# Eight sandwiched layers on one core: attention scores two tiles ahead, a norm one batch later, a clamp on GpSimd and experts' up products three units ahead

## The chip, the cores and the metric

One core of a Trainium2 chip runs the whole network in one program. The metric is the device time of that program in microseconds: the median of three runs.

## The reference

`x` has 8 sequences of 512 tokens of width 128, all in float32. Each of eight layers computes `x = x + layernorm(f(layernorm(x)))`. The `f` are, in order:

0. attention with 16 heads of width 8, RMS-normed queries and keys, and a causal window of 32 tokens
1. a gated ternary layer: `silu(x·w1·s1) * (x·w2·s2)`, two square layers of width 512 with GELU, and a last product to width 128
2. causal attention with one head
3. 32 experts, the best 4 of each token, width 128: `glu = min(a, 7)`, `lin = clip(b, -7, 7)`, `glu * sigmoid(1.702 glu) * (lin + 1)`
4. a gated delta rule with its own feed-forward layer
5. 8 experts, best 2, width 512, `silu(a) * b`
6. full attention with rotated positions
7. 8 experts, best 2, width 512, ReLU

## The kernel before

Each layer is a stage: a block in which five engines run their own instruction streams, tied by semaphores, with a barrier at its end. A batch is one sequence: `B = 8`, of `TB = 4` tiles of 128 tokens. The stream `x` stays in SBUF through all stages. There is no planner: the order on every engine is written out by hand, and every wait is in program order, so what stands behind a waiting instruction waits too. Between VectorE instructions that depend on each other, `Chain.link` (L47) adds a wait on the engine's own semaphore.

**Layer norms.** `Norm.dve_stats` (L127) takes statistics on VectorE, `pool_rstd` (L140) the power -0.5 on GpSimd, and `dve_apply` (L147) applies both on VectorE. `Post.dve_add` adds the normed result to `x`.

**Stage 0, `stage_attn0`** is unrolled over 32 tiles `n = 4b + t`. Per tile: `scores` on TensorE into PSUM banks 0 and 1 (L1006); `masked` on VectorE (L1199 adds the mask, L1202 takes the maxima); `shifted` on GpSimd (L946); `probs`, the exp, on ScalarE (L1120); `transposes` on TensorE (L1015); `probs_turned` on ScalarE (L1124); `values` on TensorE (L1028); `weighted` on VectorE. Around them the next batch is prepared: `turn_input`, `project`, `unscaled`, `squares`, `mean_squares`, `roots`, `scaled` (L1192), `turn` (L986), `queries`, `keys` (L1107, eight copies of 128x512), `project_v`, and batch b-1's output is projected and added (`result`, L1213). `scores(n+1)` is issued one tile ahead of `transposes(n)`. Banks 2 and 3 serve the projections, the turns and the output in turn.

**Stage 1, `stage_ffn0`** loops over batches. TensorE: eight up products (L354, a pair of 128x512 halves of w1 and w2 for each of four `m`, in banks 0 to 3), then two square layers of 16 products each (L363), between them the transposes of the next batch's normed input, and at last 16 products of 128x128 (L376). ScalarE: silu (L401) and GELU (L409). VectorE: the gated product (L443), then the next batch's first norm, then the wait for L376, the scaling (L451), the post norm and the add to `x` (L293), and only then the next batch's first gated product.

**Stages 3, 5 and 7, `stage_moe`** loop over batches, with 32 units unrolled in each. A unit is one 128-wide slice of hidden width: `up(u + LAG)`, two products of 128x512 (L607; one in the ReLU kind), then `down(u)`, four products of 128x128 (L617). `LAG` is 2. Four PSUM banks hold two units of up products. The routing and norms of the next batch are put between units (`AT_...`). In stage 3 every unit is an expert, so VectorE adds every unit's result into `acc` (`collect`, L784, four instructions). The nonlinearity of stage 3 is: ScalarE ta (L708), tc (L710), tb (L713); VectorE td = (ta - 7)*tc (L811) and, on the same engine, the clamp tb = min(tb - 8, 6) (L812); GpSimd h = td*tb (L544). In stage 5 it is one ScalarE and one VectorE instruction.

Of the kernel before, what the change touches and what calls it, by code (L numbers as in the profile page):

```python
# [164 lines left out]
class Pre:  # L165
# [62 lines left out]

    def dve_second(self, v, ch, b):
# [75 lines left out]
def stage_ffn0(core):  # L305
# [11 lines left out]
    free = [s(f"bank{i}_free") for i in range(4)]  # L317
    t_ready = [s(f"silu{i}_ready") for i in range(2)]
# [4 lines left out]
    with nc.Block() as block:  # L323
# [5 lines left out]
        def _(g):  # L329
# [3 lines left out]
            with g.Fori(0, B) as b:  # L333
                ch.reset()
                pre.pool(g, ch, b + 1)
                post.pool(g, ch)

        @block.tensor
        def _(pe):
            st.wait_loads(pe)  # L340
            pre.seed_pe(pe)
            for i in range(3):
                pe.sem_inc(h_free[i], 1)
            pre.pe(pe, 0)
            with pe.Fori(0, B) as b:
                pe.wait_ge(pre.xT_ready, 1)
                pe.sem_clear(pre.xT_ready)
                xb = c.xT[:, bass.ds(b * L, L)]
                for m in range(HC):
                    for k, w in enumerate((w1, w2)):  # L350
                        i = (2 * m + k) % 4
                        pe.wait_ge(free[i], 1)
                        pe.sem_clear(free[i])
                        pe.matmul(c.ps[i][:], w[:, m * P:(m + 1) * P], xb, start=True,  # L354
                                  stop=True).then_inc(ready[i], 1)
                for n, w in enumerate((h1, h2)):
# [11 lines left out]
                    if n == 0:  # L368
                        pre.pe(pe, b + 1)
                pe.wait_ge(h_ready[2], HC)  # L370
# [9 lines left out]
            for i in range(4):  # L380
                pe.wait_ge(free[i], 1)
                pe.sem_clear(free[i])
            pe.wait_ge(y_free, 1)
            pe.sem_clear(y_free)
            pre.drain_pe(pe)

        @block.scalar
        def _(a):
# [3 lines left out]
            a.sem_inc(free[2], 1)  # L392
            pre.act(a, 0)
            with a.Fori(0, B) as b:
                for m in range(HC):
                    i = 2 * m % 4
                    a.wait_ge(ready[i], 1)
                    a.sem_clear(ready[i])
                    a.wait_ge(t_free[m % 2], 1)
                    a.sem_clear(t_free[m % 2])  # L400
                    a.activation(t_s[:, m % 2, :], c.ps[i][:], ACT.Silu, scale=s1[:, m:m + 1]).then_inc(t_ready[m % 2], 1)  # L401
                    a.drain().then_inc(free[i], 1)
                for n, sc in enumerate((g1, g2)):
# [8 lines left out]
                    if n == 0:  # L412
                        pre.act(a, b + 1)
            pre.drain_act(a)
# [8 lines left out]
        def _(v):  # L423
# [8 lines left out]
            pre.dve(v, ch, 0)  # L432
            with v.Fori(0, B) as b:
                ch.reset()
                v.wait_ge(h_free[0], 1)
                v.sem_clear(h_free[0])
                for m in range(HC):
                    i = (2 * m + 1) % 4
                    v.wait_ge(ready[i], 1)
                    v.sem_clear(ready[i])  # L440
                    v.wait_ge(t_ready[m % 2], 1)
                    v.sem_clear(t_ready[m % 2])
                    v.scalar_tensor_tensor(hid[0][:, m, :], c.ps[i][:], s2[:, m:m + 1], t_s[:, m % 2, :],  # L443
                                           ALU.mult, ALU.mult).then_inc(h_ready[0], 1)
                    d = v.drain()
                    d.then_inc(free[i], 1)
                    v.sem_inc(t_free[m % 2], 1)
                pre.dve(v, ch, b + 1)
# [4 lines left out]
                v.sem_inc(y_free, 1)  # L453
                post.dve_stats(v, ch, lambda t: y[:, t, :])
                post.dve_add(v, ch, b, lambda t: y[:, t, :])
            pre.drain_dve(v)
            v.wait_ge(h_free[0], 1)
            v.sem_clear(h_free[0])
# [15 lines left out]
LAG, DEPTH = 2, 4  # L474


def stage_moe(core, tag, E, topk, inner, eps, residual, kind):
# [4 lines left out]
    FC = UNITS // E  # L482
    relu, silu, glu7 = kind == "relu", kind == "silu", kind == "glu7"
# [33 lines left out]
    td_ready = [s(f"td{i}_ready") for i in range(DEPTH)]  # L517
    y_ready = [s(f"y{i}_ready") for i in range(2)]
# [9 lines left out]
    with nc.Block() as block:  # L528
# [5 lines left out]
        def _(g):  # L534
# [12 lines left out]
            for u in range(LAG):  # L547
                hidden(u)
            with g.Fori(0, B) as b:
                ch.reset()  # L550
                for u in range(UNITS):
# [6 lines left out]
                    hidden((u + LAG) % UNITS)  # L558
# [4 lines left out]
        def _(pe):  # L563
# [71 lines left out]
            for u in range(LAG):  # L635
                up(u, c.xT[:, 0:L])
            with pe.Fori(0, B) as b:
                xb, xb_next = c.xT[:, bass.ds(b * L, L)], c.xT[:, bass.ds((b + 1) * L, L)]
                for u in range(UNITS):
# [8 lines left out]
                    if u + LAG == UNITS:  # L648
                        next_batch()
                    up((u + LAG) % UNITS, xb if u + LAG < UNITS else xb_next)  # L650
                    down(u)
            for u in range(LAG):
# [18 lines left out]
        def _(a):  # L671
# [22 lines left out]
            def front(u):  # L694
# [9 lines left out]
                if silu:  # L704
# [5 lines left out]
                a.activation(tc[:, j, :], ta[:, j, :], ACT.Sigmoid, scale=-1.702, bias=c1[:])  # L710
# [3 lines left out]
                             scale=-1.0).then_inc(t_ready[j], 1)  # L714
                a.drain().then_inc(a_free[2 * k + 1], 1)

            for u in range(LAG):
                front(u)
            with a.Fori(0, B) as b:
                ch.reset()  # L720
                for u in range(UNITS):
# [6 lines left out]
                    front((u + LAG) % UNITS)  # L728
# [3 lines left out]
        def _(v):  # L732
# [65 lines left out]
            def front(u):  # L798
# [9 lines left out]
                if glu7:  # L808
                    v.wait_ge(t_ready[j], 1)
                    v.sem_clear(t_ready[j])  # L810
                    v.scalar_tensor_tensor(td[:, j, :], ta[:, j, :], 7.0, tc[:, j, :], ALU.subtract, ALU.mult)  # L811
                    v.tensor_scalar(tb[:, j, :], tb[:, j, :], 8.0, 6.0, ALU.subtract, ALU.min).then_inc(td_ready[j], 1)  # L812
# [25 lines left out]
            for u in range(LAG):  # L838
# [2434 lines left out]
```

## Time and profile before

| | |
|---|---|
| median of 3 runs | 6248.97 us (6245.62 to 6252.19) |
| profiled execution | 6221.95 us, span 6220.1 us |
| stage 0, from 11 to 381 us | 370 us |
| stage 1, from 381 to 762 us | 381 us |
| stage 3, from 888 to 1755 us | 867 us |
| stage 5, from 4568 to 5307 us | 739 us |
| VectorE's L1199 of tiles 12 and 16 | start at 180.18 and 221.21 us |
| last L1199 of stage 0 | starts at 361.15 us |

The stages end in a barrier, so the time is the sum of the stages, and each has its own limit. Whole-program busy shares mix them; they are read in windows of one batch.

### The profile page before, as it was taken

The page shows a single profiled execution, that of the slowest core. Times are in us where ns is not written, and L with a number is a line of the kernel's source. Part 1 is how long each engine was busy: PE and PEld are TensorE (multiplying, and loading weights), DVE is VectorE, ACT ScalarE, POOL GpSimd, SP SyncE. Part 2 cuts the span into 40 slices and gives each one's busy share as a digit, 9 for nine tenths or more (in the row PEclk, how much of TensorE's full clock was granted, in tenths as well). Part 3 has the DMA queues.
Part 4 walks back from the last instruction along what each step waited for, and adds up shares of the span by engine and source line. Part 5 has one row for each costly group of instructions (what it writes and reads, how often), then busy time and mean ns, then how long its engine had stood idle before and what let it go on. Part 6 is the DMA issues. An engine that isn't in the chain of part 4 may idle for free. (4 is left out here: it accounts for less than half of the span.)

```text
span 6220.1 us, 182529 instructions
## 1 busy us (share of the span) xinstructions
PE 5232.3 (84%) x72132; PEld 3776.6 (61%) x72132; DVE 3558.8 (57%) x9531; ACT 2288.6 (37%) x4072; POOL 2504.0 (40%) x2788
## 2 busy tenths in 40 slices
PE   4568868888848888898888888898679999787998
PEld 2334345555536777777777777777346666576776
DVE  4631268787865565555565565565545545685333
ACT  3532236666623333333333333333222333111333
POOL 1210014444436666666666666666300000573000
PEclk8789989999969999999999999999789999898999
DMA  0000010000000000000000000000010000000000
GB/s 19 2 20 0 2 42 1 0 0 0 0 7 11 11 11 12 12 13 12 11 12 11 11 12 11 11 12 11 7 42 0 0 0 0 4 1 28 0 0 13
DMA packets 29562, 58.05 MB, mean 9 GB/s; under 512 B 7312, under 2 KB 14240, under 8 KB 28704
## 3 DMA queue, kind: packets, MB, share of 16 engines
q1 hardware_dynamic: 28960, 48.86, 2.6%
q8 instruction: 520, 8.52, 0.6%
q14 instruction: 82, 0.67, 0.0%
HBM read 46.75 MB, written 2.10 MB: 8 GB/s over the span
## 5 line engine op out<-in xcount | busy, mean ns | idle before, releaser
L617 PEld LDWEIGHTS psum<-m_wd,m_h 128*128 128x128 f32 x6144 | 805.6, 192 | 485.4 <-issue 484.3
L617 PE MATMUL psum<-m_wd,m_h 128*128 128x128 f32 x6144 | 819.6, 277 | 95.3 <-remote 69.6
L2183 POOL TENSOR_TENSOR e_kd<-e_kd,e_tail 128x512 f32<-128x512 f32 x325 | 368.7, 1135 | 567.7 <-PE psum L2290 554.2
L607 PE MATMUL psum<-xT,m_wa 128*128 (+1 forms) x1032 | 544.3, 610 | 8.4 <-remote 8.4
L607 PE MATMUL psum<-xT,m_wb 128*128 (+1 forms) x1032 | 532.8, 598 | 0.0
L784 DVE SCALAR_TENSOR_TENSOR m_acc<-psum,m_combine,m_acc 128x128 f32<-128x128 f32 x1440 | 403.3, 342 | 224.0 <-PE psum L617 211.0
L544 POOL TENSOR_TENSOR m_h<-m_td,m_tb 128x512 f32<-128x512 f32 x258 | 328.6, 1274 | 468.6 <-DVE m_tb L812 468.6
L2320 PE MATMUL psum<-e_T,e_N 64*64 64x32 f32 x10400 | 407.1, 232 | 67.7 <-remote 66.3
L2320 PEld LDWEIGHTS psum<-e_T,e_N 64*64 64x64 f32 x10400 | 370.6, 148 | 113.2 <-issue 110.0
L2290 PE MATMUL psum<-e_kd,e_k 64*64 64x64 f32 x10400 | 420.1, 237 | 0.3
L143 POOL TENSOR_SCALAR m_post_rstd<-m_post_mv 128x4 f32<-128x4 f32 x27 | 6.2, 228 | 990.7 <-DVE m_post_mv L133 990.7
L2290 PEld LDWEIGHTS psum<-e_kd,e_k 64*64 64x64 f32 x10400 | 372.4, 149 | 6.9 <-issue 1.2
L805 DVE SCALAR_TENSOR_TENSOR m_h<-psum,m_bb,m_ta 128x512 f32<-128x512 f32 x258 | 193.2, 749 | 308.4 <-ACT m_ta L705 305.2
L607 PEld LDWEIGHTS psum<-xT,m_wb 128*128 128x128 f32 x1032 | 199.3, 193 | 253.5 <-issue 253.5
L705 ACT ACTIVATE m_ta<-psum,m_ba 128x512 f32<-128x512 f32 x258 | 177.2, 687 | 458.9 <-PE psum L607 458.8
L2341 PE MATMUL psum<-e_Z,e_TT 64*64 64x32 f32 x8320 | 296.7, 221 | 25.0 <-DVE e_Z L2693 21.1
L2585 ACT ACTIVATE e_T<-psum 128x256 f32<-128x256 f32 x325 | 125.6, 386 | 514.4 <-PE psum L2341 514.4
L2693 DVE COPY e_Z<-psum 64x256 f32<-64x256 f32 x325 | 135.9, 418 | 301.8 <-PE psum L2320 301.5
L2341 PEld LDWEIGHTS psum<-e_Z,e_TT 64*64 64x64 f32 x8320 | 267.5, 135 | 48.7 <-issue 33.5
L699 ACT ACTIVATE m_h<-psum,m_ba 128x512 f32<-128x512 f32 x258 | 177.3, 687 | 288.3 <-PE psum L600 288.3
L2177 POOL TENSOR_TENSOR e_k<-e_k,e_tail 128x256 f32<-128x256 f32 x390 | 281.2, 721 | 0.0
L600 PE MATMUL psum<-m_normed,m_wa 128*128 128x512 f32 x516 | 268.9, 604 | 6.2 <-remote 6.2
(434 smaller groups left out, 11884.4 us busy)
## 6 DMA issues: line engine op xcount, KB each, us to landing
e_w<-in_e_w SPq DMA_DIRECT2D x66, 321.0 KB, 2.9
m_wa<-in_m_wa SPq DMA_DIRECT2D x12, 512.0 KB, 7.5
m_wd<-in_m_wd SPq DMA_DIRECT2D x12, 512.0 KB, 8.7
m_wb<-in_m_wb SPq DMA_DIRECT2D x8, 512.0 KB, 8.8
f_h<-in_f_h SPq DMA_DIRECT2D x2, 1024.0 KB
out<-x SPq DMA_DIRECT2D x1, 2048.0 KB, 8.7
f_w<-in_f_w SPq DMA_DIRECT2D x3, 256.0 KB
g_w<-in_g_w SPq DMA_DIRECT2D x3, 256.0 KB
```

The source lines that it names most:

```text
L544: g.tensor_tensor(h[:, j, :], td[:, j, :], tb[:, j, :], ALU.mult).then_inc(h_ready[j], 1)
L600: pe.matmul(c.ps[u % 4][:], wa[q][:, j, :], nrm[:, e % 2, :], start=True, stop=True).then_inc(a_ready[u % 4], 1)
L607: pe.matmul(c.ps[i][:], w[q][:, j, :], xb, start=True, stop=True).then_inc(a_ready[i], 1)
L617: r = pe.matmul(c.ps[4 + e % 2][:, t * P:(t + 1) * P], h[:, u % DEPTH, t * P:(t + 1) * P], wd[u // UQ][:, u % UQ, :], start=(m == 0 and t ...
L699: a.activation(h[:, j, :], c.ps[u % 4][:], ACT.Relu, bias=ba[:, u:u + 1]).then_inc(h_ready[j], 1)
L784: r = v.scalar_tensor_tensor(to[:, t, :], c.ps[4 + e % 2][:, t * P:(t + 1) * P], comb[:, t, e:e + 1], acc[:, t, :], ALU.mult, ALU.add)
L805: v.scalar_tensor_tensor(h[:, j, :], c.ps[2 * k + 1][:], bb[:, u:u + 1], ta[:, j, :], ALU.add, ALU.mult).then_inc(h_ready[j], 1)
L2177: return g.tensor_tensor(even(k[:], m), even(src[:], m), gate, ALU.mult)
L2183: return g.tensor_tensor(both_odd(dst[:], m), both_odd(src[:], m), gate.unsqueeze(1).broadcast_to((P, 2, nb, m)), ALU.mult)
L2290: r = pe.matmul(c.psum[half(h), G_, chunk(u)], keys[half(h), chunk(u)], both_odd(gated[half(h), :, chunk(u)], 1 << l), start=True, stop=True)
L2320: r = pe.matmul(c.psum[half(1 - h), Z_, u * HC:(u + 1) * HC], N[half(h), l - 1, chunk(u)], even(T[half(h), chunk(u)], 1 << l), start=True, ...
L2341: r = pe.matmul(even(c.psum[half(h), T_, chunk(u)], 1 << l), left[half(h), chunk(u)], Z[half(h), u, :], start=False, stop=False, skip_grou ...
```

## The change

- Stage 0: `scores`, `masked` and `shifted` run two tiles ahead of `transposes` instead of one. Every step of the next batch is moved: `project` and `unscaled` to tile 3 of two batches before, `mean_squares`, `roots`, `scaled` and `turn` to tile 0, `queries` and `keys` to tile 1, `project_v` and `values` to tile 2. A batch's result, norm and add come two batches later instead of one. The input's transposes use bank 3.
- Stage 1: TensorE issues the first pair of up products of the next batch before L376 of this one; VectorE does the first gated product of the next batch at the end of the iteration; scaling, post norm and add of a batch are done in the next iteration, after its gated products.
- Stages 3 and 5: `up` runs three units ahead, with the same four banks and four buffers.
- Stage 3: the clamp is a GpSimd instruction ahead of the product, with a semaphore of its own from ScalarE. The wait of td no longer covers tb.

The core of the diff:

```diff
 stage_ffn0, TensorE
+            up(0, c.xT[:, 0:L])
             with pe.Fori(0, B) as b:
+                for m in range(1, HC):
+                    up(m, c.xT[:, bass.ds(b * L, L)])
...
+                up(0, c.xT[:, bass.ds((b + 1) * L, L)])
                 pe.wait_ge(h_ready[2], HC)
 stage_ffn0, VectorE
+            with v.Fori(1, B) as b:
+                ch.reset()
+                for m in range(1, HC):
+                    gated(m)
+                pre.dve_first(v, ch, b + 1)
+                scaled()
                 post.dve_stats(v, ch, lambda t: y[:, t, :])
+                pre.dve_last(v, ch, b + 1)
+                post.dve_add(v, ch, b - 1, lambda t: y[:, t, :])
+                first_gated()
 stage_moe
+    lag = 2 if kind == "relu" else 3
...
+                g.wait_ge(tb_ready[j], 1)
+                g.sem_clear(tb_ready[j])
+                ch.link(g.tensor_scalar(tb[:, j, :], tb[:, j, :], 8.0, 6.0, ALU.subtract, ALU.min))
                 g.wait_ge(td_ready[j], 1)
                 g.sem_clear(td_ready[j])
                 g.tensor_tensor(h[:, j, :], td[:, j, :], tb[:, j, :], ALU.mult).then_inc(h_ready[j], 1)
...
-                    v.tensor_scalar(tb[:, j, :], tb[:, j, :], 8.0, 6.0, ALU.subtract, ALU.min).then_inc(td_ready[j], 1)
 stage_attn0, TensorE
             for n in range(N):
                 b, t = n // TB, n % TB
+                if t == 3 and b + 2 < B:
+                    project(b + 2)
+                if n + 2 < N:
+                    scores(n + 2)
+                if t == 0 and b >= 2:
+                    output(b - 2)
                 if t == 2 and b + 1 < B:
+                    project_v(b + 1)
                 if n:
                     values(n - 1)
+                if t == 0 and b + 2 < B:
+                    turn_input(b + 2)
+                transposes(n)
                 if t == 0 and b + 1 < B:
+                    turn(b + 1)
+                if t == 3 and b:
+                    turn_output(b - 1)
 stage_attn0, ScalarE
                 if t == 1 and b + 1 < B:
                     queries(b + 1)
+                    keys(b + 1, range(2))
                 if n + 1 < N:
                     probs(n + 1)
                 if t == 0 and b + 1 < B:
+                    roots(b + 1)
...
+                    keys(b + 1, range(2, 6))
...
+                    values(b + 1)
...
+                    squares(b + 2)
+                probs_turned(n)
+                if t == 1 and b + 1 < B:
+                    keys(b + 1, range(6, HP))
 stage_attn0, VectorE
+                if t == 0 and b + 1 < B:
                     mean_squares(b + 1)
+                if t == 3 and b + 2 < B:
+                    unscaled(b + 2)
+                if n + 2 < N:
+                    masked(n + 2)
+                if t == 0 and b + 1 < B:
+                    scaled(b + 1)
                 if n:
                     weighted(n - 1)
+                if t == 0 and b >= 2:
+                    result(b - 2)
+                if t == 1 and b >= 2:
                     post.dve_stats(v, ch, lambda t: y[:, t, :])
```

## Rows read from the trace of the kernel before

**Rows 1.** The page's head, whole execution.

```profile
span 6220.1 us, 182529 instructions
...
PE 5232.3 (84%) x72132; PEld 3776.6 (61%) x72132; DVE 3558.8 (57%) x9531; ACT 2288.6 (37%) x4072; POOL 2504.0 (40%) x2788
```

**Rows 2.** Windows of one batch: block attention, ternary, clamped experts, silu experts.

```profile
core 0: us, PE busy (x) PEld busy (x) DVE busy (x) ACT busy (x) POOL busy (x), PEclk, DMA share, GB/s
180.18:221.21 41.03, 23.24 (x460) 15.20 (x460) 24.47 (x49) 20.62 (x25) 10.11 (x8) 0.79 0.00 1
533.41:577.82 44.41, 39.65 (x116) 18.93 (x116) 9.12 (x31) 11.41 (x15) 2.53 (x4) 1.00 0.00 0
1230.80:1333.60 102.80, 90.48 (x409) 55.96 (x408) 82.24 (x255) 68.15 (x103) 44.49 (x38) 0.98 0.00 0
4775.90:4863.50 87.60, 87.07 (x410) 55.81 (x409) 44.37 (x127) 26.63 (x38) 3.79 (x6) 1.00 0.00 0
```

**Rows 3.** Waits in that attention batch: total, times, longest (us).

```profile
PE psum L986 <- DVEq L1215: 6.5, 1, 6.5
...
PE psum L1006 <- ACT a_kz L1107: 5.9, 1, 5.9
```

**Rows 4.** Groups by line, that batch: busy us, mean ns, idle before.

```profile
L946 POOL TENSOR_TENSOR a_probs<-a_probs,a_max 128x1024 f32<-128x1024 f32 x4 | 7.6, 1900 | 30.6 <-DVE a_max L1202 30.6
...
L1199 DVE TENSOR_TENSOR a_probs<-psum,a_window 128x1024 f32<-128x1024 f32 x4 | 4.9, 1223 | 10.0 <-PE psum L1006 10.0
...
L155 DVE TENSOR_SCALAR a_post_z<-a_y,a_post_mv,a_post_rstd 128x128 f32<-128x128 f32 x4 | 1.1, 334 | 0.0
```

**Rows 5.** Timeline of a ternary batch: start, us, what, idle before.

```profile
538.48 0.69 DVE L293 TENSOR_TENSOR x<-x,f_post_z 128x512 f32 x1 [0.15 <-DVE f_post_z L155]
539.95 0.75 DVE L443 SCALAR_TENSOR_TENSOR f_hid<-psum,f_s,f_silu 128x512 f32<-128x512 f32 x1 [0.78 <-remote]
...
540.90 2.84 PE L354 MATMUL psum<-xT,f_w 128*128 x6 [2.10 <-DVEq L445]
...
543.58 13.90 PE L363 MATMUL psum<-f_hid,f_h 128*128 128x512 f32 x32
...
573.84 3.83 PE L376 MATMUL psum<-f_w,f_hid 128*128 128x128 f32 x32 [1.08 <-remote]
```

**Rows 6.** Groups by line in one batch of the clamped experts.

```profile
L544 POOL TENSOR_TENSOR m_h<-m_td,m_tb 128x512 f32<-128x512 f32 x32 | 40.8, 1274 | 55.6 <-DVE m_tb L812 55.6
L617 PE MATMUL psum<-m_wd,m_h 128*128 128x128 f32 x256 | 34.9, 280 | 11.8 <-remote 8.2 <-POOL m_h L544 3.6
L784 DVE SCALAR_TENSOR_TENSOR m_acc<-psum,m_combine,m_acc 128x128 f32<-128x128 f32 x124 | 34.7, 341 | 1.0 <-remote 0.7
...
L811 DVE SCALAR_TENSOR_TENSOR m_td<-m_ta,m_tc 128x512 f32<-128x512 f32 x32 | 22.2, 694 | 15.6 <-ACT m_tb L713 12.6 <-remote 2.8
...
L812 DVE TENSOR_SCALAR m_tb<-m_tb 128x512 f32<-128x512 f32 x33 | 13.8, 418 | 0.0
```

**Rows 7.** GpSimd's groups over the whole trace.

```profile
L2177 POOL TENSOR_TENSOR e_k<-e_k,e_tail 128x256 f32<-128x256 f32 x390 | 281.2, 721 | 0.0
...
L2193 POOL COPY e_hs<-xT 128x512 f32 (+1 forms) x66 | 40.5, 613 | 0.3 <-POOL e_N L2227 0.3
```

**Rows 8.** Timeline in the clamped experts, VectorE and GpSimd.

```profile
1242.65 2.11 DVE L155 TENSOR_SCALAR m_post_z<-m_done,m_post_mv,m_post_rstd 128x128 f32<-128x128 f32 x4
1242.90 1.27 POOL L544 TENSOR_TENSOR m_h<-m_td,m_tb 128x512 f32<-128x512 f32 x1 [1.05 <-DVE m_tb L812]
...
1251.97 0.23 POOL L143 TENSOR_SCALAR m_pre_rstd<-m_pre_mv 128x4 f32<-128x4 f32 x1
...
1252.28 1.04 POOL L144 TENSOR_TENSOR m_pre_rstd<-m_pre_rstd,mhalf 128x4 f32<-128x4 f32 x1
```

**Rows 9.** Timeline in the delta-rule stage, same two engines.

```profile
2640.52 0.69 DVE L2756 SCALAR_TENSOR_TENSOR e_kqn<-e_kn,e_be 128x512 f32<-128x512 f32 x1
2640.57 1.12 POOL L2177 TENSOR_TENSOR e_k<-e_k,e_tail 128x256 f32<-128x256 f32 x1
```

More of the change, by code:

```diff
@@ L317, in stage_ffn0 @@
     free = [s(f"bank{i}_free") for i in range(4)]
+    gate_ready = [s(f"gate{i}_ready") for i in range(2)]
     t_ready = [s(f"silu{i}_ready") for i in range(2)]
@@ L332, in _ @@
             pre.pool(g, ch, 0)
-            with g.Fori(0, B) as b:
+            pre.pool(g, ch, 1)
+            with g.Fori(1, B) as b:
                 ch.reset()
@@ L336, in _ @@
                 post.pool(g, ch)
+            post.pool(g, ch)
         @block.tensor
@@ L392, in _, with silu @@
             a.sem_inc(free[2], 1)
+            def silu(m):
+                i = 2 * m % 4
+                a.wait_ge(ready[i], 1)
+                a.sem_clear(ready[i])
+                a.wait_ge(t_free[m % 2], 1)
+                a.sem_clear(t_free[m % 2])
+                a.activation(t_s[:, m % 2, :], c.ps[i][:], ACT.Silu, scale=s1[:, m:m + 1]).then_inc(t_ready[m % 2], 1)
+                a.drain().then_inc(free[i], 1)
             pre.act(a, 0)
+            silu(0)
             with a.Fori(0, B) as b:
[L395 to L402, printed above, removed]
+                for m in range(1, HC):
+                    silu(m)
                 for n, sc in enumerate((g1, g2)):
@@ L413, in _ @@
                         pre.act(a, b + 1)
+                silu(0)
             pre.drain_act(a)
@@ L431, in _, with gated, first_gated, scaled @@
                 v.sem_inc(t_free[i], 1)
-            pre.dve(v, ch, 0)
-            with v.Fori(0, B) as b:
-                ch.reset()
+            def gated(m):
+                i = (2 * m + 1) % 4
+                v.wait_ge(gate_ready[i // 2], 1)
+                v.sem_clear(gate_ready[i // 2])
+                v.wait_ge(t_ready[m % 2], 1)
+                v.sem_clear(t_ready[m % 2])
+                v.scalar_tensor_tensor(hid[0][:, m, :], c.ps[i][:], s2[:, m:m + 1], t_s[:, m % 2, :],
+                                       ALU.mult, ALU.mult).then_inc(h_ready[0], 1)
+                d = v.drain()
+                d.then_inc(free[i], 1)
+                v.sem_inc(t_free[m % 2], 1)
+            def first_gated():
                 v.wait_ge(h_free[0], 1)
                 v.sem_clear(h_free[0])
[L437 to L448, printed above, removed]
+                gated(0)
+            def scaled():
                 v.wait_ge(y_ready, 1)
@@ L517, in stage_moe @@
     td_ready = [s(f"td{i}_ready") for i in range(DEPTH)]
+    tb_ready = [s(f"tb{i}_ready") for i in range(DEPTH)]
     y_ready = [s(f"y{i}_ready") for i in range(2)]
@@ L546, in _ @@
             pre.pool(g, ch, 0)
-            for u in range(LAG):
+            for u in range(lag):
                 hidden(u)
@@ L634, in _ @@
             next_batch()
-            for u in range(LAG):
+            for u in range(lag):
                 up(u, c.xT[:, 0:L])
@@ L837, in _ @@
                 make_normed(1, 0)
-            for u in range(LAG):
+            for u in range(lag):
                 front(u)
@@ L1132, in _ @@
             copy_input(0)
+            copy_input(1)
             squares(0)
@@ L1237, in _ @@
             masked(0)
+            masked(1)
+            unscaled(1)
+            input_stats(2)
+            input_norm(2)
             for n in range(N):
```

169 lines of the change are left out of this document (86 added, 83 removed).

## Prediction

> **What bounds the kernel now.** The page's head first [rows 1]: TensorE is busy 84% of the span, but that is a mean over stages with different limits, and each stage ends in a barrier. So I read windows of one batch in each stage that the diff touches [rows 2]. The reader is to see four different cases. In block attention (41.03 us a batch) no engine is busy more than 60%: VectorE 24.47, TensorE 23.24, ScalarE 20.62, GpSimd 10.11. The stage is bound by a chain. In the ternary layer (44.41 us) TensorE is busy 39.65: near its floor, with single gaps. In the clamped experts (102.80 us) TensorE has 90.48, VectorE 82.24, GpSimd 44.49. In the silu experts (87.60 us), whose TensorE work is almost the same, TensorE is busy 87.07 and never waits. That number is the floor for the clamped experts too.
>
> Then the waits inside each window. In attention VectorE waits 10.0 us in three of four tiles for the scores (L1199) [rows 4]; TensorE waits 6.5 us before it turns the queries and keys, and 5.9 us for the spread keys [rows 3]. One tile of lookahead doesn't cover scores, mask, maxima, 1.90 us on GpSimd and the exp, and the next batch's preparation stands in the same line. In the ternary layer TensorE has two gaps of a size: 2.10 us before the third up pair, since VectorE first ends the post norm (add at 538.48) and only then the first gated product at 539.95, and 1.08 us before L376, for the last GELU [rows 5]. In the clamped experts GpSimd's product waits 55.6 us a batch for the clamp on VectorE, and TensorE's L617 idles 11.8 us [rows 6].
>
> **Attention.** No instruction is added in a steady batch; the order changes. Scores get a whole tile more, so the 10.0 us at L1199 should go, save where the scores themselves are late. What is late next: `turn` waits for `scaled`, which follows the masked tile on VectorE, and the scores of the next tile are queued behind `turn` on TensorE; I take 2 us. The first scores of the next batch wait for all eight copied keys, which ScalarE interleaves with an exp and a turned tile: 2.5 us. Against 6.5 and 5.9 before [rows 3]. VectorE's own 24.47 plus 2 for handovers between dependent instructions is the floor under that: 24.5 + 2 + 2 + 2.5 = 31 us. TensorE's 23.24, at a mean clock of 0.79, stays under it [rows 2]. 41.03 - 31 = 10 us for each of the seven batches that prepare a next one: -70. The end pays: one more batch's result, statistics, power, apply and add stand after the last tile (the apply is 1.1 us [rows 4], the power 1.04 and the add 0.69 [rows 5, 8]), about 5 us, and about as much goes to the longer start. Attention: -60. Bounds: 26.5 us a batch (no stall left) gives -92; 35 us (the two key waits keep most of their length) gives -32.
>
> **Ternary layer.** The post norm moves behind the gated products, so 2.10 goes; the up pair, work that has to be done anyway, fills the 1.08 before L376, less some 0.3 for TensorE's drain ahead of it: -2.9 us a batch. VectorE's 9.12 busy us and GpSimd's 2.53 [rows 2] have 27 us of square products to hide under (two times 13.90 [rows 5]). Eight batches: -23. The first batch has no post norm in its way (+2.1), and after the last a pair of no use is computed: four instructions at 13.90/32 = 0.43 us, +1.7. Together -19; from -14 (the drain and the pair's start cost 1 us a batch) to -25.
>
> **Experts three units ahead.** Silu experts: TensorE never waits, so nothing is to be won. In both stages one more unit of the next, unused batch is computed: 4 * 0.43 = 1.7 us each, +3.4 together. Below nothing is excluded for the silu stage, since its batch is 100% TensorE.
>
> **The clamp.** VectorE loses 33 clamps, 13.8 us a batch [rows 6], and has 68.4 left. A unit's latency from up to down may now be three units instead of two, so bursts of routing and norms no longer stop TensorE at once. GpSimd gains 32 clamps of 128x512. No row shows that one. From below: the copy of 128x512, 613 ns [rows 7]; from above: the two-input product of the same size, 1274 ns [rows 6]. The clamp has one input like the copy and one more arithmetic step, so I take 0.65, nearest the copy. Then GpSimd has per unit 0.65 + 1.27, a link of 0.08 (from 1251.97 + 0.23 to 1252.28 [rows 8]) and some 0.15 for two waits: 2.15 us, times 32 = 69; three powers with their adds, 1.35 each, 4; 73.
>
> But VectorE and GpSimd don't run freely beside each other. Four applies that take 1.1 us [rows 4] took 2.11 beside a GpSimd product [rows 8], and GpSimd's 128x256 product, 721 ns on average [rows 7], took 1.12 us beside a VectorE instruction with two SBUF inputs [rows 9]. L811 is of that kind (ta and tc). So each unit's L811 costs GpSimd up to 0.4: 32 * 0.4 = 13, and norms and copies some 4. GpSimd: 90 us a batch, just over TensorE's floor of 87.6. With bursts not wholly hidden I take 93. (102.8 - 93) * 8 = -79. Bounds: the floor, -122; a clamp of 0.94, halfway to the product, adds 9.3 us: 102.3, or -4; at 1.27 with nothing overlapped, see the last rival.
>
> The Trainium skill, page "SBUF — State Buffer", section "Who interferes with whom", says that a VectorE instruction with two SBUF inputs and a GpSimd instruction that reads SBUF exclude each other for their whole length. Rows 9 agree in kind, with 0.4 us of 0.69 paid. The page speaks against this change: the clamp leaves VectorE's list but not the common resource; what that gives when taken whole is the first rival. The skill's "GPSIMD Engine Reference", section "Engine selection", calls one-input instructions there roughly line-rate; by that the clamp would be an estimated 0.43 us and a start cost, near my 0.65, and no run here shows it yet.
>
> **Sum.** -60 - 19 + 3.4 - 79 = -155, from the profiled execution's 6221.95 us (span 6220.1 and 1.9 around it): 6067. The median of the runs is 27 us above the profiled one, so 6249 - 155 = 6094 us.
>
> **Rivals.**
> 1. *The pair excludes itself wholly.* Per unit 0.69 (L811) + 0.65 + 1.27 + 0.23 gaps = 2.84; times 32 = 91, plus 4 for powers and 4 for norms: 99 us. The clamped experts give only -30: 6143 us. For it: rows 8 and 9. Against: in rows 9 part of GpSimd's start lay under the other's work.
> 2. *Attention's preparation still rules.* `scaled`, `turn`, keys and scores of a batch remain a line. Half of the 12.4 us of waits [rows 3] and the lookahead for nothing: 37.5 us a batch, -25 for the stage, 6129 us. For it: the waits of rows 3 are as long as L1199's. Against: each step has a tile of its own now.
> 3. *The lookahead does it all.* The clamped experts reach TensorE's floor, -122: 6051 us. For it: VectorE 68.4 and GpSimd 73 both lie under 87.6. Against: the overlap above.
> 4. *Slower.* The clamp on GpSimd costs as much as the product and overlaps nothing: 0.69 + 1.27 + 1.27 + 0.23 = 3.46 a unit, 111 + 8 = 119 us a batch, +128; with the other parts' -76, 6301 us. It decides from a batch of 112.3 us on, that is a clamp of 1.06 us. Against: the copy of 613 ns.
> 5. *It doesn't do what it says:* a new semaphore order makes TensorE wait elsewhere and all three stages stay within 0.2%. Little speaks for it, since TensorE's order does change.
>
> **How the numbers follow.** Chances: forecast 0.58, rival 1 0.16, rival 2 0.10, rival 3 0.09, rival 4 0.05, rival 5 0.02. The forecast's own range, from the bounds of its parts taken two at a time, is 6060 to 6130. To leave out no more than 2 in 10 the range has to reach past rivals 1 to 3, with the attention bound of -92 beside a part of rival 3 below: 6035 to 6185. Faster by over 0.2% (12.5 us, about what a measurement of this kernel can tell from no change) 0.93, within 0.02, slower 0.05.
>
> **What would show it.** In the changed profile: an attention batch (four L1199) of 28 to 34 us, with VectorE the busiest and L1199's wait mostly gone; TensorE's wait before `turn` near 2 us. A ternary batch of 41 to 42 us, with no gap over 0.5 inside the up products. A clamped batch of 90 to 96 us, a GpSimd clamp of 0.6 to 0.75 us, GpSimd busier than VectorE, L811 longer than its 694 ns where it meets GpSimd. A silu batch of 87.6 again. The prediction is wrong if the clamp takes over 0.95 us, if L811 and the product strictly alternate with gaps, or if attention stays over 36 us a batch.

## The result and the profile after

The changed kernel takes 6284.2 us (median of 4 runs, 6280.7 to 6289.0) against 6247.3 us before (4 runs, 6243.6 to 6252.2): a ratio of 1.0065, 95% interval 1.0049 to 1.0082. It is slower by 0.65%. The prediction was 6094 us, range 6035 to 6185, with 0.05 for slower. The sign was wrong.

The page's head and the row of the clamp, after:

```profile
span 6284.2 us, 183125 instructions
...
PE 5277.6 (84%) x72144; PEld 3773.8 (60%) x72144; DVE 3531.7 (56%) x9276; ACT 2292.1 (36%) x4078; POOL 3030.4 (48%) x3048
...
L588 POOL TENSOR_SCALAR m_tb<-m_tb 128x512 f32<-128x512 f32 x259 | 513.8, 1984 | 40.8 <-ACT m_tb L761 19.1
```

TensorE's busy time and share are almost those of [rows 1]. The new row is the case: the clamp on GpSimd takes 1.98 us on average. The stages, measured between barriers in both traces:

| stage | before | after | difference | predicted |
|---|---|---|---|---|
| 0, block attention | 369.7 | 327.0 | -42.7 | -60 |
| 1, ternary | 381.0 | 358.5 | -22.5 | -19 |
| 3, clamped experts | 867.2 | 989.3 | +122.1 | -79 + 1.7 |
| 5, silu experts | 739.0 | 741.1 | +2.1 | +1.7 |
| the others | | | +5.1 | 0 |

The sum is +64 of the two profiled spans. The profiled execution of before lay 25 us under its own median and that of after 2 us over its own, so the medians differ by 37. Of the others' +5.1, 7 us are in the delta rule (layer 4), whose code is the same. In the profiles of all the kernels with that code but the last one below it took 2605 to 2628 us (2619 before, 2626 after), so that is scatter. Three of the four parts went in the direction predicted; the fourth outweighs them.

Windows of one batch, after, in the order of [rows 2]:

```profile
core 0: us, PE busy (x) PEld busy (x) DVE busy (x) ACT busy (x) POOL busy (x), PEclk, DMA share, GB/s
164.35:198.01 33.66, 21.15 (x450) 14.42 (x452) 24.24 (x50) 20.31 (x25) 10.13 (x8) 0.85 0.01 2
616.50:657.80 41.30, 39.34 (x118) 19.09 (x117) 8.89 (x32) 11.42 (x15) 2.64 (x4) 1.00 0.00 0
1212.50:1330.30 117.80, 97.23 (x409) 55.62 (x408) 79.20 (x223) 68.13 (x102) 109.23 (x71) 0.97 0.00 0
4840.80:4928.40 87.60, 86.97 (x410) 55.71 (x409) 44.33 (x126) 26.64 (x38) 3.80 (x6) 1.00 0.00 0
```

A clamped batch takes 117.80 us and GpSimd is busy in 109.23 of them, against 44.49 before. VectorE went from 82.24 down to 79.20 only, for two reasons. The 13.8 us of clamps overlapped their neighbours on VectorE: with the clamps taken out of the trace of before, its busy time in that batch falls by 8.1 us. And a td takes 0.86 us on average instead of 694 ns [rows 6], 5.3 us a batch. The groups of that batch:

```profile
L588 POOL TENSOR_SCALAR m_tb<-m_tb 128x512 f32<-128x512 f32 x33 | 65.4, 1981 | 2.8
L591 POOL TENSOR_TENSOR m_h<-m_td,m_tb 128x512 f32<-128x512 f32 x32 | 41.2, 1288 | 5.6 <-remote 5.3 <-POOL m_tb L588 0.4
L664 PE MATMUL psum<-m_wd,m_h 128*128 128x128 f32 x256 | 37.6, 292 | 19.9 <-POOL m_h L591 16.5 <-remote 3.4
...
L859 DVE SCALAR_TENSOR_TENSOR m_td<-m_ta,m_tc 128x512 f32<-128x512 f32 x32 | 27.5, 860 | 27.7 <-ACT m_tc L757 25.0 <-remote 2.6
```

L588 is the clamp, L591 the product (L544 before), L664 `down` (L617 before), L859 td (L811 before). GpSimd now waits 8 us ahead of these two instructions where it waited 55.6 [rows 6]. TensorE waits 19.9 us ahead of `down` instead of 11.8, and 16.5 of it for GpSimd's product instead of 3.6. The timeline of one unit between bursts (a burst is the VectorE work of norm, routing or sum that stands between two units):

```profile
1082.73 1.92 POOL L588 TENSOR_SCALAR m_tb<-m_tb 128x512 f32<-128x512 f32 x1
...
1083.16 0.73 DVE L859 SCALAR_TENSOR_TENSOR m_td<-m_ta,m_tc 128x512 f32<-128x512 f32 x1 [1.39 <-ACT m_tc L757]
...
1084.83 1.27 POOL L591 TENSOR_TENSOR m_h<-m_td,m_tb 128x512 f32<-128x512 f32 x1 [0.18 <-remote]
...
1086.18 1.92 POOL L588 TENSOR_SCALAR m_tb<-m_tb 128x512 f32<-128x512 f32 x1
...
1086.25 1.15 PE L664 MATMUL psum<-m_wd,m_h 128*128 128x128 f32 x8 [0.57 <-POOL m_h L591]
```

Clamp 1.92, gap 0.18, product 1.27, gap 0.08: 3.45 us from one clamp to the next. 32 times that is 110.4 us, with the three powers 114. Clamps and products stretched beside VectorE (means of 1.98 and 1.29 us, for 1.92 and 1.27) add 3. TensorE's `down` starts 0.15 us after the product's end and had waited 0.57 us. VectorE's td (L859), which began 0.43 us into the clamp, took 0.73 us, hardly more than its 694 ns.

Attention, the waits of the batch of the first window:

```profile
PE psum L1042 <- DVEq L1276: 6.7, 1, 6.7
DVE a_probs L1260 <- PE psum L1062: 6.5, 2, 4.1
...
PE psum L1062 <- ACT a_kz L1164: 4.5, 1, 4.5
```

L1042 is `turn`, L1062 the scores, L1260 the mask's add. Before, the three were 6.5, 10.0 and 5.9 [rows 3, 4]. The batch went from 41.03 to 33.66, and the wait before `turn` is still there. Its timeline says what stands before it:

```profile
181.60 1.90 POOL L995 TENSOR_TENSOR a_probs<-a_probs,a_max 128x1024 f32<-128x1024 f32 x1 [3.07 <-DVE a_max L1263]
...
182.41 2.17 DVE L1253 TENSOR_TENSOR a_qk<-a_raw,a_rstd 128x1024 f32<-128x1024 f32 x1
...
185.46 0.69 DVE L1274 TENSOR_TENSOR a_y<-psum,a_bo 128x512 f32<-128x512 f32 x1
...
186.35 1.94 PE L1042 MATMUL psum<-ident,a_qk 128*128 128x128 f32 x8 [6.65 <-DVEq L1276]
```

`scaled` (L1253) took 2.17 us beside GpSimd's L995, where its median before was 1.44, and `turn` was released by the semaphore of L1276, behind L1274: that is `result`, which reads batch b-2's output out of PSUM bank 2 and so frees it for `turn`. VectorE's list places it behind `scaled` and `weighted`; it ended at 186.15.

Ternary layer, TensorE in one batch:

```profile
560.81 1.98 PE L359 MATMUL psum<-xT,f_w 128*128 x4 [0.53 <-remote]
...
562.63 3.73 PE L392 MATMUL psum<-f_w,f_hid 128*128 128x128 f32 x32
...
567.19 5.41 PE L359 MATMUL psum<-xT,f_w 128*128 x12 [0.82 <-remote]
```

Of the two gaps of [rows 5], 2.10 and 1.08 us, there are 0.53 us before the early pair and 0.82 before the rest of the up part.

### The profile page after: what moved, and what is told of

Same layout as the page of the kernel before. It is cut to its first block and busy times, and to the rows that moved or that the text cites. A ratio compares the mean times of both kernels' runs of the same rounds, so it can differ in the third digit from the quotient of the medians.

```text
span 6284.2 us, 183125 instructions
## 1 busy us (share of the span) xinstructions
PE 5277.6 (84%) x72144; PEld 3773.8 (60%) x72144; DVE 3531.7 (56%) x9276; ACT 2292.1 (36%) x4078; POOL 3030.4 (48%) x3048
## 5 line engine op out<-in xcount | busy, mean ns | idle before, releaser
L664 PEld LDWEIGHTS psum<-m_wd,m_h 128*128 128x128 f32 x6144 | 797.8, 193 | 606.1 <-issue 604.9
L664 PE MATMUL psum<-m_wd,m_h 128*128 128x128 f32 x6144 | 840.1, 280 | 162.7 <-POOL m_h L591 135.5
L588 POOL TENSOR_SCALAR m_tb<-m_tb 128x512 f32<-128x512 f32 x259 | 513.8, 1984 | 40.8 <-ACT m_tb L761 19.1
L591 POOL TENSOR_TENSOR m_h<-m_td,m_tb 128x512 f32<-128x512 f32 x259 | 334.9, 1293 | 45.5 <-remote 42.4
L859 DVE SCALAR_TENSOR_TENSOR m_td<-m_ta,m_tc 128x512 f32<-128x512 f32 x259 | 221.6, 856 | 232.2 <-ACT m_tc L757 210.7
L752 ACT ACTIVATE m_ta<-psum,m_ba 128x512 f32<-128x512 f32 x259 | 178.0, 687 | 460.7 <-PE psum L654 460.6
L755 ACT ACTIVATE m_ta<-psum,m_ba 128x512 f32<-128x512 f32 x259 | 177.9, 687 | 348.7 <-PE psum L654 348.4
```

Source lines behind the costliest of these rows:

```text
L588: ch.link(g.tensor_scalar(tb[:, j, :], tb[:, j, :], 8.0, 6.0, ALU.subtract, ALU.min))
L591: g.tensor_tensor(h[:, j, :], td[:, j, :], tb[:, j, :], ALU.mult).then_inc(h_ready[j], 1)
L664: r = pe.matmul(c.ps[4 + e % 2][:, t * P:(t + 1) * P], h[:, u % DEPTH, t * P:(t + 1) * P], wd[u // UQ][:, u % UQ, :], start=(m == 0 and t ...
```

## The experiments

All ran after the prediction. By then the theory was that the clamp's own duration on GpSimd sets the batch (T1). It had two rivals: the third unit of lookahead costs something itself (T2), or VectorE and GpSimd exclude each other, so that the place of the clamp matters more than its length (T3).

**Clamp back on VectorE, all else as changed.**

```diff
 GpSimd
-                g.wait_ge(tb_ready[j], 1)
-                g.sem_clear(tb_ready[j])
-                ch.link(g.tensor_scalar(tb[:, j, :], tb[:, j, :], 8.0, 6.0, ALU.subtract, ALU.min))
 VectorE
                     v.scalar_tensor_tensor(td[:, j, :], ta[:, j, :], 7.0, tc[:, j, :], ALU.subtract, ALU.mult)
+                    v.tensor_scalar(tb[:, j, :], tb[:, j, :], 8.0, 6.0, ALU.subtract, ALU.min)
...
```

The semaphores of ta, tb and td are again those of the kernel before.

> The changed kernel with the clamp on VectorE again; attention, ternary layer and three units ahead stay. Theory A (the clamp's 1.95 us on GpSimd is the whole loss, and three units ahead let the bursts on VectorE pass): a clamped batch falls from 118 to 88 to 95 us, the stage from 989 to 750 to 810, the program to 6045 to 6105 us. Rival B (VectorE bounded the stage and lookahead gives nothing): a clamped batch of 103 us as before the change, the program at 6160 us.

Measured: 6175.3 us (4 runs) against 6231.1 before, ratio 0.9906 [0.9890, 0.9923]. Clamped stage 880.9 us, batches of 104.0 to 106.4. So the clamp's move cost 108 us of the stage, and the third unit by itself gained nothing: 105 us a batch against 103 before, near the 103 of rival B and far from the 88 to 95 of theory A. Its waits in one batch:

```profile
DVE m_td L855 <- ACT m_tb L757: 14.2, 19, 2.2
PE psum L661 <- remote: 12.7, 7, 3.5
```

and its timeline between bursts:

```profile
1104.02 0.67 ACT L757 ACTIVATE m_tb<-psum,m_bb 128x512 f32<-128x512 f32 x1
...
1104.91 1.02 PE L651 MATMUL psum<-xT,m_wb 128*128 x2
...
1105.01 0.70 DVE L855 SCALAR_TENSOR_TENSOR m_td<-m_ta,m_tc 128x512 f32<-128x512 f32 x1 [0.26 <-ACT m_tb L757]
...
1105.76 1.05 PE L661 MATMUL psum<-m_wd,m_h 128*128 128x128 f32 x8
...
1105.97 1.88 DVE L153 TENSOR_SCALAR m_pre_y<-m_pre_y,m_inner_rstd 128x128 f32<-128x128 f32 x4
```

VectorE takes td of a unit (L855, 1105.01) 0.32 us after ScalarE's last output for it (1104.02 + 0.67). A unit more of lookahead on all engines doesn't make VectorE less late. By the code its list asks for the *newest* unit before it adds the `down` results that free one of two accumulator banks, and TensorE computes that newest unit only behind an earlier `down`. TensorE then waits 12.7 us a batch at L661 without a releaser that the trace names; it isn't the product, which has rows of its own, and by the code what is left is the bank.

**The clamp alone, on the kernel before (two units ahead).** The clamp's three lines on GpSimd, the attention and ternary layers and the lookahead as before.

> The kernel before with the clamp alone moved to GpSimd, two units ahead. Theory A: GpSimd's 1.92 + 0.18 + 1.27 + 0.08 = 3.45 us a unit sets the pace whatever the lookahead: 118 to 121 us a batch, the program 6365 to 6385 us. Rival C (the loss comes from the third unit in four banks and buffers, not from the clamp): at most 105 us a batch.

Measured: 6349.6 us (one run). Clamped stage 984.6 us, batches of 117.1 to 118.7, clamp 1.92 us. With or without the third unit the batch is 118 us, as theory A said; rival C allowed 105 at most. That supports T1 and leaves nothing to T2 while GpSimd sets the pace.

**What GpSimd does in the clamp's place.** The queue, the waits and the buffers stay; only the instruction is changed. The copy leaves out the upper limit and the subtraction of 8, the one step leaves out the upper limit. The two added lines belong to one kernel each.

```diff
-                ch.link(g.tensor_scalar(tb[:, j, :], tb[:, j, :], 8.0, 6.0, ALU.subtract, ALU.min))
+                ch.link(g.tensor_copy(tb[:, j, :], tb[:, j, :]))                       # copy
+                ch.link(g.tensor_scalar(tb[:, j, :], tb[:, j, :], 8.0, None, ALU.subtract))   # one step
```

> The changed kernel with a copy on GpSimd in the clamp's place (the upper limit and the shift by 8 are left out, so the expert outputs differ). It gives the clamp the price that the prediction took. If the prediction's sum was right but for that price: copy 0.61 to 0.65 us, 90 to 95 us a batch, program 6040 to 6100 us. If the two engines exclude each other for the whole length of L859 and both GpSimd instructions (rival 1): 97 to 101 us a batch, program 6110 to 6140 us.

> The changed kernel with one arithmetic step in the clamp instead of two (the upper limit is left out). Theory D (GpSimd's price grows with each step, on top of a copy's 0.19 start): about 1.05 us, GpSimd 2.6 us a unit, 92 to 97 us a batch. Rival E (this form has one price whatever its steps): 1.9 us and 118 us a batch. Rival F (line rate for one step): 0.65 us.

Measured, one run each: copy 6137.9 us, stage 851.7, batches of 100.2 to 101.9; one step 6188.8 us, stage 905.1, batches of 106.7 to 108.1. GpSimd's group in 100 us of each, the copy's first:

```profile
L588 POOL COPY m_tb<-m_tb 128x512 f32<-128x512 f32 x32 | 24.3, 760 | 14.7 <-ACT m_tb L761 14.6
```

```profile
L588 POOL TENSOR_SCALAR m_tb<-m_tb 128x512 f32<-128x512 f32 x30 | 48.1, 1603 | 2.5
```

The medians are 0.61 us for the copy, 1.49 for one arithmetic step, 1.92 for two, and 1.27 for the two-input product; the copy's mean is 0.76, its longest 1.08. The copy's price of [rows 7] was right for the copy; the first arithmetic step adds 0.88 us to it, the second 0.43. The stage follows the duration: 101, 107, 118 us a batch. T1 holds. None of the three guesses at one step (1.05, 1.9 or 0.65 us) was right. And the copy shows the second fault of the prediction: even at the copy's price the batch is 101 us, not 93. That lies in the range given to full exclusion, rival 1 (97 to 101), so exclusion had to be looked at by itself.

T3 can be read from the changed kernel's own trace. Of its 259 td instructions (L859), some 198 began inside a clamp and took 0.74 us on average, 48 began inside a product and took 1.38, and 13 met neither and took 0.69. The averages hide what decides. Two units of it, td inside a clamp and td inside a product:

```profile
1103.61 1.92 POOL L588 TENSOR_SCALAR m_tb<-m_tb 128x512 f32<-128x512 f32 x1
...
1103.77 0.99 DVE L859 SCALAR_TENSOR_TENSOR m_td<-m_ta,m_tc 128x512 f32<-128x512 f32 x1 [0.25 <-remote]
...
1105.71 1.27 POOL L591 TENSOR_TENSOR m_h<-m_td,m_tb 128x512 f32<-128x512 f32 x1 [0.18 <-remote]
...
1106.06 1.47 DVE L859 SCALAR_TENSOR_TENSOR m_td<-m_ta,m_tc 128x512 f32<-128x512 f32 x1 [0.26 <-remote]
```

The second td ended 0.55 us after the product's end, and so did all 48 (0.545 to 0.550). Its length is what is left of the product plus 0.55 us. Before the change 96 td began inside a product too, but some 0.15 us before its end, and took 0.70. The first td ended 1.15 us after the clamp's start. So did 83 of the 90 td that began in a clamp's first 0.48 us (the other seven met longer clamps), and all that began later than 0.53 us took 0.69. Beside the copy of the kernel further down, which takes 0.61 us, a td again ended 1.15 to 1.16 us after the copy's start (50 of the 51 that began inside one). So the product excludes td until its end, and the clamp only for its first 0.6 us, as long as a copy takes, and not for the 1.3 us after that. T3 is right about the exclusion and wrong about the pace: in the changed kernel most td lie in a clamp and lose little there, and the clamp's length is what counts.

**VectorE a unit behind the others.** In this kernel the distance is a number for each pair of engines (`lag` for TensorE and ScalarE, `vlag` for VectorE and GpSimd). If the rest of the loss is VectorE's order, it should go when TensorE and ScalarE run three units ahead, but VectorE and GpSimd ask for a unit only two ahead, which is then one unit old. In the same kernel attention's `result(b - 2)` stands ahead of `scaled(b + 1)`, to see what released `turn`. The clamp is on VectorE.

```diff
     lag = 2 if kind == "relu" else 3
+    vlag = 2
 GpSimd, VectorE
-                    hidden((u + lag) % UNITS)        # and front(...)
+                    hidden((u + vlag) % UNITS)       # and front(...)
 stage_attn0, VectorE
+                if t == 0 and b >= 2:
+                    result(b - 2)
                 if t == 0 and b + 1 < B:
                     scaled(b + 1)
-                if t == 0 and b >= 2:
-                    result(b - 2)
```

> Clamp on VectorE, up products and ScalarE three units ahead, but VectorE's and GpSimd's part of a unit only two ahead, so that VectorE does not ask for the newest unit before it collects a result. Theory G (the third unit gave nothing because VectorE's list ties every collect, and with it TensorE's accumulator bank, to the newest up product): a clamped batch falls from 105 to 88 to 98 us, stage 3 from 881 to 740 to 830 us. Rival H (the two accumulator banks or VectorE's bursts themselves bound it, wherever its nonlinearity stands): 102 to 106 us. In attention the result of two batches before is read ahead of the scaling: TensorE's wait before its turn shortens by 0.7 us, a batch from 34 to 33 us, the stage by 4 to 8 us.

Measured: 6120.7 us (5 runs) against 6246.8, ratio 0.9797 [0.9781, 0.9813]. Clamped stage 833.6, batches of 99.0 to 100.4: 6 us less than with the clamp back alone. That is just short of theory G (88 to 98 us) and under rival H (102 to 106). Attention 320.1 us, 8.6 less than with the clamp back, whose attention code is the changed kernel's (328.7 there, 327.0 after). The silu experts, to which `vlag` applies as well, lost by it: 745.2 us for 741.1. Two waits of one clamped batch:

```profile
PE psum L664 <- remote: 6.1, 3, 3.0
...
DVE m_td L858 <- ACT m_tb L760: 2.6, 10, 0.3
```

and the wait before `turn`:

```profile
PE psum L1043 <- DVEq L1256: 5.0, 1, 5.0
```

TensorE's wait for a bank fell from 12.7 to 6.1 us, VectorE's for ScalarE from 14.2 to 2.6. `turn` now waits for L1256, `scaled`, 5.0 us instead of 6.7: `result` was what held it last, and `scaled` is next.

**The same with the copy, and without either; all keys at once.** The copy's kernel with VectorE and GpSimd a unit behind, and then with the line taken out (both leave out the upper limit and the subtraction of 8). In both, all eight copies of the keys are made at tile 1, ahead of the next exp, and attention's `result` stands as in the changed kernel.

```diff
-                    keys(b + 1, range(2))
+                    keys(b + 1, range(HP))
```

> As the run with a copy on GpSimd in the clamp's place (upper limit and shift left out), with VectorE and GpSimd two units ahead. If theory G holds, 88 to 92 us a batch instead of 101; if the shared use of SBUF by the two engines bounds it (rival 1), 97 to 101 us. In attention all eight keys are spread before the next exp: if the keys are what the next batch's scores wait for, a batch 1 to 2 us shorter than 34; if the exp and the turned tile are, 1 us longer.

> As the run with a copy in the clamp's place and VectorE and GpSimd two units ahead, without the copy: no clamp anywhere (upper limit and shift left out). If the copy's share of the common SBUF path held that run at 99.3 us a batch, 90 to 94 us; if bursts on VectorE around the two accumulator banks did, 97 to 99.3 us.

Measured, one run each: with the copy 6095.6 us, clamped stage 833.5, batches of 99.2 to 99.4, attention 303.5 us. With nothing 6082.0, stage 800.9, batches of 94.4 to 95.7. One such batch:

```profile
core 0: us, PE busy (x) PEld busy (x) DVE busy (x) ACT busy (x) POOL busy (x), PEclk, DMA share, GB/s
1118.00:1213.70 95.70, 89.54 (x409) 56.07 (x408) 72.78 (x223) 68.16 (x103) 44.53 (x39) 0.98 0.00 0
```

and the copy beside td, of the kernel with the copy:

```profile
1106.41 1.17 DVE L862 SCALAR_TENSOR_TENSOR m_td<-m_ta,m_tc 128x512 f32<-128x512 f32 x1 [0.26 <-remote]
...
1106.97 1.08 POOL L589 COPY m_tb<-m_tb 128x512 f32<-128x512 f32 x1
```

Here both engines pay: L862, held by the rest of the product ahead of it, takes 1.17 us, and the copy, held by L862, 1.08 for its 0.61. On average td takes 0.93 us and the copy 0.86 in this kernel. By the stages (833.6 with the clamp on VectorE, 833.5 with the copy on GpSimd, 800.9 with neither) this work costs 4 us a batch on either engine, on GpSimd even at the copy's price: once VectorE's order is mended, there is nothing to be won by the move. The batch without it, 94.4 to 95.7 us, lies between the two ranges expected, so neither the copy's share nor the bursts alone hold the batch at 99.3.

The keys gave the larger part of attention: 327.0 to 303.5 us. The 4.5 us at the scores are gone from its waits, and the wait before `turn` is as it was:

```profile
PE psum L1047 <- DVEq L1277: 6.6, 1, 6.6
```

**Norms and routing behind the unit's own work.** Without any clamp a batch is still some 8 us over the floor of 87.6 [rows 2]. If that is the bursts of VectorE work put between units, the order inside a unit should matter. VectorE's `collect` and `front` go ahead of the pieces of norm and routing (clamp on VectorE, as in the kernel with VectorE behind).

> As the first run of this call, with the norm, routing and sum pieces on VectorE put behind the unit's collect and nonlinearity instead of ahead of them. If a burst costs because it stands between a finished down product and the release of its bank, 3 to 6 us a batch less than the first; if the order inside a unit is all the same, within 1 us.

Measured: 6153.7 us (one run), clamped stage 858.4, batches of 102.3 to 102.5: 3 us a batch worse. The expectation was 3 to 6 us better, or no change. The order of the burst matters, and this one is the wrong way round. That the remaining 8 us are bursts fits this, but no run removed them. A rival stands beside it, and no run tested it either: in every pass of the loop after the first, and in every kernel here, VectorE waits 3.1 to 3.5 us before the first instruction of its loop, where the silu experts of the kernel before wait 0.7 us. So the 8 us stay open.

**All that helped, together.** VectorE a unit behind in the clamped experts with the clamp on VectorE, two units of lookahead in the silu experts, all keys at once, `result` ahead of `scaled`; and the same with the clamp of 8 of the 32 units on GpSimd, where it has time.

```diff
-    lag = 2 if kind == "relu" else 3
+    lag = 3 if kind == "glu7" else 2
+    vlag = 2
+    on_pool = (3, 5, 7, 9, 12, 19, 22, 28)     # second kernel only
```

> The best of the runs so far in one kernel: clamp on VectorE, up products three and nonlinearity two units ahead in the clamped experts, silu experts two units ahead as before the change, in attention the result ahead of the scaling and all eight keys before the next exp, the ternary layer as changed. By stages 303 + 358 + 834 + 739 us beside an unchanged rest: 6085 us; if the parts are not independent, over 6100 us.

> As the combined kernel, with the clamp on GpSimd in eight of 32 units, those whose nonlinearity on VectorE follows a norm or routing piece. GpSimd has over 50 us a batch to spare and 1.92 us for each. If VectorE's bursts hold the batch at 99 us, each burst is 0.42 us shorter: 95 to 97 us a batch, 6050 to 6070 us. If GpSimd's slower clamp then is late for its own product, 99 to 102 us a batch and no gain.

Measured against 6245.1 before (9 runs): together 6090.5 us (5 runs, 6082.0 to 6095.6), ratio 0.9752 [0.9734, 0.9769], the fastest of all. Attention 295.2 us, clamped stage 833.2, silu stage 738.9. Its attention batch of 29.4 us and clamped batch of 99.1:

```profile
core 0: us, PE busy (x) PEld busy (x) DVE busy (x) ACT busy (x) POOL busy (x), PEclk, DMA share, GB/s
164.60:194.00 29.40, 19.89 (x409) 13.42 (x398) 23.76 (x50) 20.30 (x25) 9.73 (x9) 0.86 0.01 2
1123.40:1222.50 99.10, 90.22 (x409) 55.77 (x408) 83.08 (x254) 68.11 (x103) 44.51 (x38) 0.98 0.00 0
```

With eight clamps on GpSimd 6148.9 us (5 runs), ratio 0.9846 [0.9829, 0.9863]: 58 us slower than without, where a gain of some 3 us a batch, or none, was expected. In the profiled spans, 68 us apart, the clamped stage is 9 us longer (842.3 us, 100.4 a batch): the clamps moved gave nothing even where GpSimd had time. Two stages with the same code in both kernels make up the rest. The silu stage is 30 us longer (92.1 us a batch for 87.6). The delta rule is 29 us longer (2637 for 2608) in these two profiles; since it took 2605 to 2628 us in the other kernels, most of these 29 us may be scatter. The medians' 58 us less the other two stages leave 19. In the silu stage two waits stand out, both once a batch, and neither among the longest waits of the kernel together:

```profile
DVE m_combine L898 <- remote: 5.6, 1, 5.6
...
PE psum L659 <- DVEq L861: 2.7, 1, 2.7
```

L898 is the first instruction of VectorE's loop. The 5.6 us has no releaser that the trace names. Of the DMA queues in that stage, one differs. It carries instructions; the first line is of the kernel together, the second of the one with eight clamps:

```profile
q14 instruction: 4, 0.03, 0.0%
```

```profile
q14 instruction: 39, 0.32, 0.1%
```

The 35 packets more are five for each of the seven returns to the start of the loop, at the same point each time: the first of them starts at 4588.2, 4680.2 and 4772.3 us, as VectorE's wait at L898 begins. So in this kernel the silu loop has instructions loaded in each pass, and in the other not. The clamped experts' loop has as many packets a pass in every kernel, that of before too, with its 3.1 to 3.5 us at VectorE's first instruction. The coincidence in time is shown. That the load is what VectorE waits for is argued, and why the same loop needs it in one kernel and not in the other is open: no run moved the loop's code alone.

## Why the prediction was wrong, by its own steps

- **The clamp's price: the step that failed.** "From below: the copy of 128x512, 613 ns [rows 7]; from above: the two-input product of the same size, 1274 ns", and then "I take 0.65, nearest the copy." It is 1.92 us, outside both bounds, and over the 0.95 us that the prediction itself named as the sign of being wrong. The copy has no arithmetic, and a row with another kind of arithmetic isn't an upper bound for this one. The bracket went by operand counts, and the cost goes with the steps: 0.61, 1.49, 1.92 us for none, one and two. Of the clamped stage's error of 200 us, 137.6 come from here (the stage with the copy is 851.7, with the clamp 989.3). The Trainium skill, page "GPSIMD Engine Reference", section "Engine selection", calls one-input instructions on GpSimd roughly line-rate. Here that describes the copy at best; a one-input instruction with one arithmetic step takes 1.49 us, more than the two-input product's 1.27. The measurement decides.
- **"bursts of routing and norms no longer stop TensorE at once": failed too.** With the clamp back on VectorE the third unit gained nothing: the stage is 880.9 us against 867.2. VectorE's list turned the deeper lookahead into a demand for a newer unit. With VectorE left a unit behind it gave 4 us a batch. The batch at the copy's price is 101, not 93: this term, 3 us for bursts above GpSimd's 90, was short by 8 us a batch, about 60 us. VectorE's order is 2.3 of the 8 ((851.7 - 833.5)/8). Some 4 is the whole cost of the copy there ((833.5 - 800.9)/8), part of which the sum had counted. And without any clamp the batch is already 94.4 to 95.7 us, above the 93 that was to hold with it. The 68.4 us left to VectorE was short as well, since its clamps overlapped their neighbours: the kernel without a clamp has VectorE busy in 72.78.
- **Overlap: the rows were read right, the rule was not whole.** The prediction charged each td with 0.4 us on GpSimd. With the clamp, GpSimd pays 0.09 a unit (0.06 on the clamp, 0.03 on the product), and td 0.16. With the copy and VectorE behind, each pays about 0.24 on average. The Trainium skill, page "SBUF — State Buffer", section "Who interferes with whom", has such a VectorE instruction contend with a GpSimd instruction that reads SBUF, and calls it an exclusive lock. The product agrees: all 48 td that began inside one ended 0.55 us after it. The clamp agrees for its first 0.6 us and not for the rest of its 1.92.
- **Rival 4** had the right outcome, 119 us a batch against 118 measured, and by luck: it took 1.27 for the clamp and no overlap; measured is 1.92 and almost full overlap. For the same reason its pivot, "a clamp of 1.06 us", is wrong. With one step the clamp takes 1.49 us, the batch 107, and the program was still faster than before (6188.8 against 6231.1 us, one run). The prediction's own pivot in batch time, 112.3 us, lies between the 107 of one step and the 118 of two. An estimate between those two points puts it at a clamp of 1.7 us. Its chance of 0.05 was low because the copy was taken as evidence against it. **Rival 1**'s 99 us a batch is what the mended kernels measure, but not by its account. The clamp on VectorE gives the same 99.1, and there a product hardly holds a td (mean 0.70 us); 94.4 to 95.7 of the 99 are there with no clamp anywhere.
- **Attention: the waits named were the right ones, their sizes were off.** -60 predicted, -42.7 measured. The wait at L1199 was to be mostly gone and shrank from 10.0 to 6.5 us. The two waits named as next were undersized: 6.7 us before `turn` (2 predicted) and 4.5 for the keys (2.5). A batch is 33.7 us and not 31. `result`, moved to two batches later, stands in the path to `turn`: the prediction named only `scaled`, which also took 0.7 us longer than before. Start and end cost 4 us, not 10.
- **Ternary: right in its sum.** -22.5 against -19, 41.3 us a batch against 41 to 42. The gap before the early pair is 0.5 where 0.3 was taken, for which no row stood. The sign "no gap over 0.5 inside the up products" failed: there are 0.82 us before the rest of them.
- **Extra units, silu experts: right.** +2.1 against +1.7, 87.60 us a batch again.

The three parts without the clamp sum to -63 in the trace. With the clamp where it was, the whole is 0.94% faster than before.

## What to carry to other kernels

An instruction that the trace has not shown has no sure price between two neighbours that differ in kind. If it would be issued 32 times a batch on the engine that everything then waits for, the price at which the sign turns matters more than the likeliest price. Here the chance of passing it was read off the nearest row, which was of another kind. In the clamped experts lookahead paid only once the engine that frees the buffers asked for an older unit than the engines that fill them, and in the silu experts that same setting cost 4 us: each engine and each loop has its own distance. When a step is moved later, list what else frees the bank or buffer that the next step needs; a moved `result` can hold up a `turn` that has nothing to do with it.

## What the runs showed of the hardware

- On GpSimd, 128x512 in float32 within SBUF: copy 0.61 us, subtract 1.49, subtract and min 1.92, product of two tensors 1.27. On VectorE subtract and min take 0.42 [rows 6].
- VectorE's td, with two SBUF inputs, takes 0.69 us alone. When it began inside GpSimd's two-input product it ended 0.545 to 0.550 us after the product did (48 cases, 1.38 us on average).
- When it began in the first 0.48 us of the 1.92 us clamp it mostly ended 1.15 us after the clamp's start; later than 0.53 us in, it took 0.69. Beside a copy of 0.61 us it ended 1.15 to 1.16 us after the copy's start. The clamp excludes it for as long as a copy does.
- The clamped experts' loop has five instruction packets a pass and a wait of 3.1 to 3.5 us at VectorE's first instruction, in every kernel. The silu experts' loop, with the same code, had none of these packets in the kernel together, and five a pass with a wait of 5.4 to 5.6 us in the kernel with eight clamps on GpSimd; its stage took 30 us more.
